# Macaron block on one core: the second FFN's opening in another order, with unread products in TensorE's rests

## The reference

```
x = x + 0.5 * ffn(layernorm(x))
x = x + attention(layernorm(x))      # 16 heads of 8, relative shift, softmax over 512 keys
x = x + 0.5 * ffn(layernorm(x))

ffn(h): h = layer_norm(h, g1, b1) @ ternary(w1).T + b1'      # 128 -> 512
        h = gelu(h); h = layer_norm(h, g2, b2)               # over the 512 hidden
        return h @ ternary(w2).T + b2'                       # 512 -> 128
```

## Time and profile before

| | us |
|---|---|
| median of 3 runs | 432.4 |
| profiled execution, own time | 432.4 |
| its span in the profile | 430.6 |
| DVE busy | 392.2 (91%) |
| PE busy | 351.8 (82%) |
| ACT busy | 264.1 (61%) |
| POOL busy | 176.0 (41%) |

### The profile page before, as it was taken

The page is one execution under the profiler, slowest core; times in us unless marked ns, Lnnn a source line. Parts: engine busy times, 40 slices in busy tenths (PEclk is TensorE's granted clock), DMA queues, the critical chain, the costliest instruction groups (busy, mean ns, idle before and its releaser), DMA issues.

```text
span 430.6 us, 18108 instructions
## 1 busy us (share of the span) xinstructions
PE 351.8 (82%) x7344; PEld 288.4 (67%) x7344; DVE 392.2 (91%) x565; ACT 264.1 (61%) x642; POOL 176.0 (41%) x216
## 2 busy tenths in 40 slices
PE   1887798785989788897888978889798897984893
PEld 1666675663878677686776867768687686961683
DVE  8879888459999999999999999999999999958695
ACT  1687365336566666666666666666666666633990
POOL 7444756549313415144150431505325053204562
PEclk9999899988899999999999999999999999996899
DMA  7004257574221323213132131322313242010002
GB/s 220 1 2 174 70 144 233 145 203 113 42 70 35 83 45 69 72 34 82 34 73 66 38 81 30 78 64 40 80 22 87 67 76 36 23 52 2 0 26 73
DMA packets 58853, 31.01 MB, mean 72 GB/s; under 512 B 35470, under 2 KB 57454, under 8 KB 58702
## 3 DMA queue, kind: packets, MB, share of 16 engines
q1 hardware_dynamic: 57470, 29.18, 26.5%
q0 software_dynamic: 672, 0.49, 0.8%
q10 hardware_dynamic: 672, 0.80, 0.7%
HBM read 19.44 MB, written 10.88 MB: 70 GB/s over the span
## 4 chain that ended last, share of the span: by engine, by line
DVE 55%; issue 20%; PE 12%; ACT 5%; POOL 3%; SPq 2%; DVEq 1%; DMA 0%; POOLq 0%; ACTq 0%
DVE pT L989 27%; DVE negmax L975 19%; PE pair L1097 2%; DVE xh L796 2%; DVE sqsum L908 1%; PE pair L1055 1%; PE pair L1243 1%; ACT v_rep L679 1%; ACT v_rep L691 1%; DVE x L922 1%; POOL grs L521 1%; PE pair L1199 1%; DVE stat L786 1%; DVE pT L956 1%; PE pair L1284 1%
## 5 line engine op out<-in xcount | busy, mean ns | idle before, releaser
L727 ACT ACTIVATE probs<-pair,negmax 128x512 f32<-128x512 f32 x256 | 173.9, 684 | 104.7 <-DVE negmax L975 104.7
L975 DVE TENSOR_REDUCE negmax<-pair 128x2 f32<-128x1024 f32 x128 | 152.1, 1188 | 6.3 <-PE pair L1216 6.3
L989 DVE STREAM_TRANSPOSE pT<-probs 128x1024 f32<-128x1024 f32 x128 | 157.0, 1227 | 0.4 <-ACT probs L727 0.4
L1199 PE MATMUL pair<-stage_k,stage_c 128*32 128x512 f16 x1024 | 115.5, 399 | 33.0 <-ACT probs L727 30.0
L1205 PE MATMUL pair<-stage_z,stage_q 128*32 128x512 f16 x1024 | 112.5, 387 | 0.0
L584 POOL TENSOR_TENSOR xh<-rowsum,xh 128x16 f32<-128x16 f32 x15 | 43.6, 2904 | 162.8 <-ACT probs L727 162.8
L1216 PE MATMUL pair<-stage_z,stage_q 128*32 128x446 f16 (+59 forms) x1024 | 102.0, 282 | 0.0
L1211 PE MATMUL pair<-stage_z,stage_q 128*32 128x488 f16 (+56 forms) x1024 | 99.5, 278 | 0.0
L1243 PE MATMUL pair<-pT,v_diag 128*32 128x128 f32 (+1 forms) x2176 | 90.5, 267 | 0.0
L1199 PEld LDWEIGHTS pair<-stage_k,stage_c 128*32 128x32 f16 x1024 | 52.6, 140 | 46.3 <-ACT probs L727 36.2
L1243 PEld LDWEIGHTS pair<-pT,v_diag 128*32 128x32 f32 x2176 | 69.3, 111 | 2.1
(11 more groups left out here) (118 smaller groups left out, 366.4 us busy)
## 6 DMA issues: line engine op xcount, KB each, us to landing
stage_z<-z_scratch SPq DMA_DIRECT2D x16, 254.0 KB
stage_q<-qs_scratch SPq DMA_DIRECT2D x116, 24.0 KB
qs_scratch<-pT SPq DMA_DIRECT2D x9, 256.0 KB, 2.6
stage_z<-z_scratch SPq DMA_DIRECT2D x16, 128.0 KB
kc_scratch<-pT SPq DMA_DIRECT2D x8, 256.0 KB
stage_z<-z_scratch SPq DMA_DIRECT2D x16, 127.5 KB
stage_c<-qc_scratch SPq DMA_DIRECT2D x61, 32.0 KB
stage_k<-kc_scratch SPq DMA_DIRECT2D x15, 128.0 KB
```

The source lines that it names most:

```text
L727: nc.scalar.activation(probs[:, q % 6, :], score_pair(q // 2)[:, q % 2, :], ACT.Exp, bias=negmax[:, q % 8:q % 8 + 1], accum_out=rowsum[:, ...
L975: nc.vector.tensor_reduce(negmax[:, 2 * n % 8:2 * n % 8 + 2], score_pair(n)[:, :, :], AX.X, ALU.max, negate=True).then_inc(max_ready, 1)
L989: nc.vector.transpose(pT[:, par, 2 * n:2 * n + 2, :].rearrange("p a s -> p (a s)"), probs[:, 2 * n % 6:2 * n % 6 + 2, :].rearrange("p a s ...
L1199: mm(bank[32 * j:32 * j + 32, :], all_rows[:, 32 * j:32 * j + 32], stage_k[:, par, :], start=True, stop=False, skip_group_check=True)
```

## The change

Two things. First, a function `fill(bank, count)` makes PE run `count` matmuls of 512 columns on the float16 weights into a bank that nobody reads from afterwards (the next owner overwrites it). It is called in three places: 10 products into bank 6 between `bo_ready` and the wait for head 0's loads, 13 into bank 1 after the last `direct`, and 8 into bank 1 between the transpositions of batch 0 and the second FFN.

Second, the tail's order. DVE makes `xh` of batch 1 and the low half of batch 0 before it turns to batches 2 and 3; the low half of batch 0 leaves POOL's list. The first hidden product (high half) waits only for the float16 evacuation, the second for DVE's subtraction (`first_low`). The transpositions of batch 1 move behind the first hidden block.

```diff
+IDLE_FIRST, IDLE_ADD, IDLE_TURN = 10, 13, 8
@@ POOL
             ln_rstd(2, 1)
-            ln_low(2, 0)
             ln_rstd(2, 2)
@@ DVE
-            for b in range(B):
+            for b in range(2):
                 add_attention(b)
                 ln_stats(2, b)
-                if b:
-                    ln_xhats(2, b - 1)
-            ln_xhats(2, B - 1)
+            ln_xhats(2, 0)
+            ln_xhats(2, 1)
+            dve.wait_ge(ln[2]["xT"], 2)
+            nc.vector.tensor_tensor(xT_low[:, 0:S], xT[:, 0:S], xT_high[:, 0:S], ALU.subtract).then_inc(first_low, 1)
+            for b in range(2, B):
+                add_attention(b)
+                ln_stats(2, b)
+            for b in range(2, B):
+                ln_xhats(2, b)
             ffn(1)
@@ PE, ffn
-                        pe.wait_ge(ln[2 * f]["xT_low"], g + 1)
+                        if f == 1 and n == 0:
+                            pe.wait_ge(ln[2]["xT"], 1)
+                        elif f == 0 or g:
+                            pe.wait_ge(ln[2 * f]["xT_low"], g + 1 - f)
...
                         mm(ps[n % 2], w1T[:, k], xT_high[:, tokens], start=True, stop=False)
+                        if f == 1 and n == 0:
+                            pe.wait_ge(first_low, 1)
                         mm(ps[n % 2], w1T[:, k], xT_low[:, tokens], start=False, stop=True).then_inc(s["hid"], 1)
...
-                    if n in TURN_STEPS[f] and (f == 0 or n):
+                    if n in TURN_STEPS[f]:
@@ PE
+            def fill(bank, count):
+
+                for _ in range(count):
+                    mm(ps[bank], w1T[:, 0:128], w1T[:, :], start=True, stop=True)
...
+            fill(6, IDLE_FIRST)
             pe.wait_ge(staged_pool, 16 * LOADS_POOL)
             head(0, 0, 16 * LOADS_EVEN, True)
...
+            fill(1, IDLE_ADD)
             for t in range(4):
                 ln_turn(2, t)
-            for t in range(4):
-                ln_turn(2, 4 + t)
+            fill(1, IDLE_TURN)
             ffn(1)
```

More of the change, by code:

```diff
@@ L192, in macaron_kernel @@
               for f in range(2)]
+        first_low = sem("first_low")
         pos_mm = sem("pos_mm")
```

## The result

The changed kernel takes 429.82 us (median of 6 runs, 429.07 to 430.73) against 432.49 of before (6 runs): a ratio of 0.9941, 95% interval 0.9925 to 0.9956, 2.67 us less. A second set of 6 runs beside other runs of before gave 0.9949 (0.9935 to 0.9963). The forecast was 429.0 with a range of 427.8 to 431.2.

A forecast was written before the change was run, and what follows sets the result against it. The prediction took attention to be bound by DVE and the tail by its first gelu. Head 0's 1.4, head 1's 0.3 and the tail's 1.7 sum to 3.4 us, so 432.4 becomes 429.0, range 427.8 to 431.2.

The forecast's parts named there:

- What bounds it: Attention is bound by DVE and ends earlier by exactly what DVE starts earlier; the tail gains what its first gelu gains.
- Head 0's start: Ten products before head 0's scores hold the full clock, price 0.04 us; first transposition at 91.8 instead of 93.20, 1.4 gained.
- upper bound of 1.8: Most that head 0's start could gain, in us: what the second maxima move.
- Head 1: At head 1's start, part of the first tile may run at full clock: between 0 and 0.65 us, taken as 0.3.
- The tail's order: In the tail, the new order and products bring the first gelu to 393.7 instead of 395.75, 2.05 us earlier.
- What comes late next: In the tail, POOL's subtraction beside batch 2's scalings delays ACT's evacuation; 0.3 us given back, leaving 1.7 for the tail.
- Sum: Whole kernel: 1.4 + 0.3 + 1.7 = 3.4 us gained, from 432.4 to 429.0.
- The head's start pays nothing: Rival: at head 0 the clock may not fall in other executions, so only the tail gains; 430.7 us, chance 0.13.
- The tail's products don't hold the clock: Rival: the clock falls within the tail's 8 products, gelu at 395.2, only 0.5 gained there; 430.2 us, chance 0.11.
- Slower: Rival: products at head 0 and in the tail run at 1.2 GHz, delaying both; 436.1 us, chance 0.06.
- three signs of being wrong: Attention's end moves under 1 us, a DMA releases head 1's first tile, or ACT gaps before batch 2's evacuation.
- DVE's idle 4.6 or less: Sign that the forecast holds: DVE's idle before row maxima is 4.6 us or less in all.

The follow-up runs named there:

- sum_ahead_head_one: Changed kernel with DVE's first sum of squares ahead of batch 3's scalings and 12 more products before head 1's first score tile: 429.44 us, ratio 0.9946.
- head_twenty: Changed kernel with 20 products instead of 10 ahead of head 0's loads: 432.55 us, ratio 1.0010 to the kernel before.
- head_only: Kernel before plus only the 10 products ahead of head 0's loads, old tail order and no tail products: 430.77 us, ratio 0.9967.
- order_only: Changed kernel with all three product counts at 0, leaving only the tail's new order: 430.67 us, ratio 0.9975 to the kernel before.
- no_head_products: Changed kernel without the 10 products ahead of head 0's loads, tail products kept: 431.08 us, ratio 0.9985 to the kernel before.
- head_and_order: Changed kernel without the tail's 21 products, keeping the 10 at head 0 and the new order: 428.64 us, ratio 0.9931 to the kernel before.

## Why the prediction was right, and where it was off

- **What bounds it.** Right: DVE's start sets attention's end. First transposition 1.41 earlier, first addition 1.74. "Between head 1's opening and the tail, DVE never waits" leaves out 0.37 for ACT and 2.40 for PE at attention's last products; they are the same in both kernels, but it is the second that grew in `sum_ahead_head_one` and `head_twenty`.
- **Head 0's start**, forecast 1.4 and a price of 0.04. Measured 1.41. First maxima at 89.05 (forecast 89.07), second at 90.45 (90.39), transposition at 91.79 (91.8); ten products from 85.12 to 87.44. That these times of the span agree so closely is partly luck, since the first score tile alone moved by 2 us between executions; what holds in every profile with products is 4.39 to 4.43 from the first score tile to the first transposition, against 5.61 to 6.61 without. The upper bound of 1.8 was mis-subtracted: 92.06 - 90.39 is 1.67.
- **Head 1**, forecast 0.3. Measured 292.80 - 292.47 = 0.33 between the first transposition and the first addition. The number is right by luck. I let the clock fall at the same time of the trace, with part of the first tile done at full clock; it fell at about 104.0 instead of 104.7, ahead of the first tile, whose first group took 0.65 as before. What was saved is the second wait, since the clock came back sooner. Nor is it steady: in `head_only`, `order_only` and `no_head_products` this stretch was 291.91 or 291.92, with the clock at 1.00, and in `head_and_order`, where it fell, 292.10.
- **The tail's order**, forecast 2.05 at the first gelu. Measured 2.04. That the 13 products cost nothing: right. But I gave the 8 and the 13 products no price of their own; `order_only` shows that 1.68 of the 2.04 comes without them.
- **What comes late next**: the step that was off, in its size. I let 0.3 be given back, and 1.08 was. I carried the doubled scalings through batch 2 only, where they took 1.70 and did no harm: ACT's evacuation came 397.19 - 391.97 = 5.22 after the gelu, undelayed. I did not carry them to batch 3, whose scalings meet the constant row and the next subtraction both, and ahead of DVE's first sum, which ACT's fourth square needs. The earlier trace rows had the price, 2.06 beside one operation, but not the place: that takes POOL's list followed from batch 2's statistics to batch 3's roots.
- **Sum.** 1.4 + 0.3 + 1.7 = 3.4 became 1.41 + 0.33 + 0.96 = 2.70 in the spans, 2.67 in the medians.
- **Rivals.** The head's start pays nothing: refuted by `head_only` (0.9967, interval below 1). The tail's products don't hold the clock: they hold it. That rival was also priced wrong: with no products in the tail and the clock falling, 1.68 is still gained at the first gelu (`order_only`), not 0.5. Slower, with products at half clock: not seen; but `head_twenty` shows that a late first tile is paid in full, on which its price rested. None of the three signs of being wrong came. My "DVE's idle 4.6 or less" was 4.7.

## What to carry to other kernels

Keep TensorE's clock up only where its half speed is on the path, and count the products against the rest: ten were free, ten more made the first tile 2.27 us late. When an engine's work is brought forward, follow each engine's list past the first consumer to the next buffer that is reused; here one sum of 0.68 us behind four scalings cost 1.08. The best version found keeps the change and moves that sum ahead: 427.96 us in 4 runs, 0.9898 of before (0.9884 to 0.9912).

## What was not expected of the hardware

A rest of the same length doesn't always lower the clock. In `order_only` PE rested 3.02 us ahead of head 1 and the clock stayed at 1.00, where in the changed kernel it fell in the same rest:

```profile
105.20 0.45 PE L1216 MATMUL pair<-stage_k,stage_c 128*32 128x512 f16 x4 [3.02 <-ACT probs L728]
```

```profile
104.13 0.65 PE L1216 MATMUL pair<-stage_k,stage_c 128*32 128x512 f16 x4 [3.02 <-ACT probs L728]
```

The first row is of `order_only`, the second of the changed kernel; a group of four products takes 0.45 at 2.4 GHz and 0.65 at 1.2 GHz. The stretch from first transposition to first addition was 0.9 us shorter than before in the three profiles where the clock held by itself. What makes it fall or hold is not shown. These three are different kernels, profiled once each; that single runs of one kernel differ by this, and by the landing of head 0's loads, is likely but not shown.
